# Eight experts' weights split into high and low halves: most low halves made by TensorE and ScalarE instead of VectorE

## The reference

```python
xf = x.reshape(-1, d)                            # 4096 tokens, d = 512
logits = jnp.dot(xf, w_gate)                     # E = 8 experts
top_logits, top_idx = jax.lax.top_k(logits, 2)
weights = jax.nn.softmax(top_logits, axis=-1)
sort_order = jnp.argsort(top_idx.reshape(-1))    # token copies grouped by expert
h0 = jax.lax.ragged_dot(sorted_x, wi_0, group_sizes)   # wi_0, wi_1: 8 x 512 x 256
h1 = jax.lax.ragged_dot(sorted_x, wi_1, group_sizes)
out_sorted = jax.lax.ragged_dot(silu(h0) * h1, wo, group_sizes)  # wo: 8 x 256 x 512
out = weighted sum of the two copies of each token
```

## Time and profile before

| | |
|---|---|
| time, median of 3 runs | 2045.12 us (2044.48 to 2049.25) |
| time of the profiled execution | 2043.97 us |
| its span in the profile | 2042.3 us |
| PE busy | 1773.9 us, 87% |
| DVE busy | 1737.6 us, 85% |
| ACT busy | 1341.5 us, 66% |
| POOL busy | 856.5 us, 42% |
| `route`, first instruction to last | 1606.8 to 1689.7 us of the span |
| `run_experts` | 1691.2 us to the end |

### The profile page before, as it was taken

How to read it: one execution, slowest core, us unless ns; L and a number is a source line. 1 busy time by engine, 2 the same in 40 slices (tenths; PEclk the granted TensorE clock), 3 DMA queues, 4 the chain that set the end, 5 groups by cost and what they waited for, 6 DMA issues and landing times. The chain is left out here.

```text
span 2042.3 us, 59210 instructions
## 1 busy us (share of the span) xinstructions
PE 1773.9 (87%) x24267; PEld 1226.2 (60%) x24326; DVE 1737.6 (85%) x2331; ACT 1341.5 (66%) x1933; POOL 856.5 (42%) x842
## 2 busy tenths in 40 slices
PE   3799999998999998999989999999984137999996
PEld 2567667666766676666667666767762013555553
DVE  6699999999999999999998999999994595666665
ACT  5478778877877787788768777868774332322322
POOL 5033422743282246227432822451234003766776
PEclk9899999999999999999999999999996568999998
DMA  6313424551554354445524553533332354566775
GB/s 190 112 39 83 113 67 83 127 138 45 113 128 117 68 124 127 99 83 120 143 47 102 128 126 71 124 102 82 73 67 83 105 156 140 184 203 216 247 260 190
DMA packets 205999, 246.30 MB, mean 121 GB/s; under 512 B 93668, under 2 KB 134628, under 8 KB 205728
## 3 DMA queue, kind: packets, MB, share of 16 engines
q1 hardware_dynamic: 165904, 146.43, 26.6%
q0 software_dynamic: 37952, 95.47, 18.2%
q10 hardware_dynamic: 1872, 0.55, 0.1%
HBM read 137.66 MB, written 70.79 MB: 102 GB/s over the span
## 5 line engine op out<-in xcount | busy, mean ns | idle before, releaser
L877 DVE TENSOR_TENSOR a_p_low<-a_p 128x1024 f16<-128x1024 f32 (+1 forms) x896 | 1095.6, 1248 | 91.7 <-ACT a_p L707 80.1
L707 ACT ACTIVATE a_p<-ps_s 128x1024 f32<-128x1024 f32 (+1 forms) x896 | 860.1, 965 | 284.1 <-PE ps_s L504 278.5
L504 PE MATMUL ps_s<-a_q_stack,a_k_stack 96*128 96x512 f16 (+1 forms) x1664 | 513.5, 383 | 13.7 <-ACT a_p L707 12.7
L630 PE MATMUL ps_o<-a_v,a_p 128*128 128x65 f16 (+1 forms) x6656 | 448.0, 195 | 44.2 <-ACT a_o_sums L735 21.4
L630 PE MATMUL ps_o<-a_v,a_p_low 128*128 128x65 f16 (+1 forms) x6656 | 447.2, 194 | 0.0
L630 PEld LDWEIGHTS ps_o<-a_v,a_p 128*128 128x128 bf16 (+1 forms) x6656 | 352.2, 98 | 143.5 <-DVE a_p_low L877 53.1
L541 PEld LDWEIGHTS ps_p<-wkv,a_ctx 128*128 128x128 f16 x4992 | 321.5, 98 | 143.5 <-DVE a_v L892 38.1
L541 PE MATMUL ps_p<-wkv,a_ctx 128*128 128x128 f16 x4992 | 365.7, 221 | 28.0 <-DVE a_v L892 26.7
L523 PE MATMUL ps_p<-a_ctx,wkv 128*128 128x384 f16 (+2 forms) x1536 | 349.9, 334 | 0.0
L630 PEld LDWEIGHTS ps_o<-a_v,a_p_low 128*128 128x128 f16 (+1 forms) x6656 | 317.7, 98 | 0.0
L523 PEld LDWEIGHTS ps_p<-a_ctx,wkv 128*128 128x128 f16 x1536 | 148.4, 98 | 140.4 <-issue 4.1
(11 more groups left out here) (242 smaller groups left out, 1996.4 us busy)
## 6 DMA issues: line engine op xcount, KB each, us to landing
a_k_stack<-a_k_parts SPq DMA_DIRECT2D x378, 80.0 KB, 2.2
d_ys<-f_y SPq DMA_DIRECT2D x71, 256.0 KB
a_ctx_raw<-in_ctx_dram POOLq DMA_DIRECT2D x64, 192.0 KB, 3.4
a_q_stack<-d_q_t SPq DMA_DIRECT2D x96, 128.0 KB, 4.1
a_xm<-in_x_dram SPq DMA_DIRECT2D x8, 1024.0 KB, 5.9
a_ctx_raw<-in_ctx_dram POOLq DMA_DIRECT2D x32, 256.0 KB, 4.2
d_q_t<-a_q_parts SPq DMA_DIRECT2D x32, 256.0 KB, 2.9
d_q_full<-a_xm SPq DMA_DIRECT2D x32, 256.0 KB, 2.8
```

What stands on the lines that cost most here:

```text
L504: mm = pe.matmul(t["ps_s"][s % 2][0:r, n * N:(n + 1) * N], t["k_stack"][v % 2][0:TERMS * DH, j, kt * P:kt * P + r], t["q_stack"][v % 2][0: ...
L630: mm = pe.matmul(t["ps_o"][:, q * VC:(q + 1) * VC], part[0:r, n * N + q * P:n * N + (q + 1) * P], val, start=(g == 0 and n == 0 and low == ...
L707: act.activation(t["p"][s % NP][0:r, 0:len(tiles) * N], t["ps_s"][s % 2][0:r, 0:len(tiles) * N], ACT.Exp, scale=float(DH) ** -0.5 / WSCALE ...
L877: dve.tensor_tensor(t["p_low"][s % NP][0:r, 0:n], full, high, ALU.subtract).then_inc(lows, 1)
```

## The change

The number of raw buffers goes from 3 to 4. Of the 24 low parts, VectorE keeps 8: pieces 3 and 17 to 23. The 16 others (0, 1, 2 and 4 to 16) are made in PSUM: for each half of a piece, TensorE multiplies the raw float32 half by a diagonal matrix of 64 in float32 and adds the high part times minus the identity in float16 (`subtract`), and ScalarE copies the result from PSUM to the low part as float16 (`low_piece`). Two PSUM tiles take turns, each two banks wide. GpSimd makes the two diagonal matrices at the stage's start. All engines' orders are written anew, and the stage has four semaphores more (20, were 16). Cut to its core:

```diff
-        raw = [sbuf(nc, held, f"e_raw{n}", [P, 2, 2 * FF], F32) for n in range(PIECES)]
+        raw = [sbuf(nc, held, f"e_raw{n}", [P, 2, 2 * FF], F32) for n in range(NW)]      # NW = 4
+ON_VECTOR = (3,) + tuple(range(17, PIECES * E))
+ON_TENSOR = [i for i in range(PIECES * E) if i not in ON_VECTOR]
...
+        def wait_read(eng, i):
+            if i in ON_VECTOR:
+                eng.wait_ge(split_vector, ON_VECTOR.index(i) + 1)
+            else:
+                eng.wait_ge(subtracted, ON_TENSOR.index(i) + 1)
...
+            pool.tensor_scalar(spread_32[:, :], k["id32"][:, :], WSCALE, None, ALU.mult).then_inc(diagonal, 1)
+            pool.tensor_scalar(minus_16[:, :], k["id32"][:, :], -1.0, None, ALU.mult).then_inc(diagonal, 1)
...
+            for i in range(PIECES * E):          # SyncE
+                if i >= NW:
+                    wait_read(sp, i - NW)
...
+            def high_piece(i):                   # ScalarE
+                act.wait_ge(loaded[i % NW], 32 * (i // NW + 1))
+                act.mul(weight_piece(i, 0), raw[i % NW][:, :, :], WSCALE).then_inc(high, 1)
+            def low_piece(j):
+                act.wait_ge(subtracted, j + 1)
+                act.copy(weight_piece(ON_TENSOR[j], 1), ps_low[j % 2][:, :, :]).then_inc(split_tensor, 1)
+            ready = iter(range(len(ON_TENSOR)))
+            def pieces(first, last):
+                for i in range(first, last):
+                    high_piece(i)
+                    if i in ON_TENSOR and ON_TENSOR.index(i) >= 1:
+                        low_piece(next(ready))
...
+            pieces(0, 3)
             act.wait_ge(gap_ready, 1)
             act.activation(ratio[:, :], gap[:, :], ACT.Exp, scale=1.0 / WSCALE).then_inc(ratio_ready, 1)
-            high_pieces(range(0, 4))
+            pieces(3, 13)
             for c in range(TOPK):
                 act.wait_ge(tile_ready, TOPK)
                 act.activation(mark(c, 0), tile_hot[c], ACT.Identity,
                                scale=row_1[:, 0:1]).then_inc(marked[c], 1)
-                high_pieces(range(4 + 2 * c, 6 + 2 * c))
+            pieces(13, PIECES * E)
+            for j in ready:
+                low_piece(j)
...
+            def subtract(j):                     # TensorE
+                i = ON_TENSOR[j]
+                pe.wait_ge(high, i + 1)
+                if j >= 2:
+                    pe.wait_ge(split_tensor, j - 1)
+                for h in range(2):
+                    pe.matmul(ps_low[j % 2][:, h, :], spread_32[:, :], raw[i % NW][:, h, :], start=True, stop=False)
+                    last = pe.matmul(ps_low[j % 2][:, h, :], minus_16[:, :], weight_piece(i, 0)[:, h, :], start=False, stop=True)
+                last.then_inc(subtracted, 1)
+            pe.wait_ge(diagonal, 2)
+            for j in range(3):
+                subtract(j)
             pe.wait_ge(hot_ready, 1)
...
+            for j in range(3, 12):
+                subtract(j)
             for c in range(TOPK):
                 pe.wait_ge(marked[c], 2)
...
+                for j in (range(12, 14) if c == 0 else range(14, len(ON_TENSOR))):
+                    subtract(j)
```

More of the change, by code:

```diff
@@ L1589 @@
 PIECES = 3
+NW = 4
+ON_VECTOR = (3,) + tuple(range(17, PIECES * E))
+ON_TENSOR = [i for i in range(PIECES * E) if i not in ON_VECTOR]
 VALUES = 6
@@ L1597, in route, with weight_piece @@
     with ExitStack() as held, phase(nc) as (block, sem):
-        raw = [sbuf(nc, held, f"e_raw{n}", [P, 2, 2 * FF], F32) for n in range(PIECES)]
-        loaded = [sem(f"e_loaded{n}") for n in range(PIECES)]
-        high, split = sem("e_high"), sem("e_split")
-        def weight_piece(e, n, part):
-            return t["wi"][:, e, part, 2 * n:2 * n + 2, :] if n < 2 else t["wo"][:, e, part, :, :]
+        raw = [sbuf(nc, held, f"e_raw{n}", [P, 2, 2 * FF], F32) for n in range(NW)]
+        loaded = [sem(f"e_loaded{n}") for n in range(NW)]
+        high, subtracted, split_tensor, split_vector, diagonal = (
+            sem("e_" + n) for n in ("high", "subtracted", "split_tensor", "split_vector", "diagonal"))
+        spread_32, minus_16 = sbuf(nc, held, "e_spread", [P, P], F32), sbuf(nc, held, "e_minus", [P, P], F16)
+        def weight_piece(i, part):
+            e, n = i // PIECES, i % PIECES
+            return t["wi"][:, e, part, 2 * n:2 * n + 2, :] if n < 2 else t["wo"][:, e, part, :, :]
+        def wait_read(eng, i):
[3 more added lines that the diff above has]
+                eng.wait_ge(subtracted, ON_TENSOR.index(i) + 1)
         sb = lambda name, shape, dt=F32: sbuf(nc, held, "r_" + name, shape, dt)
@@ L1645, in route @@
         ps_before, ps_total, ps_table = banks(nc, held, ["r_pb", "r_pt", "r_ps"])
+        ps_low = [held.enter_context(nc.psum_tensor(f"e_ps{n}", [P, 2, 2 * FF], F32)) for n in range(2)]
         made, spread, step, hot_ready, summed, gap_ready, ratio_ready, tile_ready, listed = (
@@ L1660, in _ @@
                                pattern=[[1, P]], channel_multiplier=-1).then_inc(made, 1)
+            pool.tensor_scalar(spread_32[:, :], k["id32"][:, :], WSCALE, None, ALU.mult).then_inc(diagonal, 1)
+            pool.tensor_scalar(minus_16[:, :], k["id32"][:, :], -1.0, None, ALU.mult).then_inc(diagonal, 1)
         @block.sync
         def _(sp):
[L1664 to L1674, removed]
+            for i in range(PIECES * E):
+                e, n = i // PIECES, i % PIECES
+                if i >= NW:
+                    wait_read(sp, i - NW)
+                for h in range(2):
+                    if n < 2:
+                        sp.dma_start(raw[i % NW][:, :, h * FF:(h + 1) * FF],
+                                     (t["wi_0"], t["wi_1"])[h][e, n * 2 * P:(n + 1) * 2 * P, :]
+                                     .rearrange("(c p) f -> p c f", p=P)).then_inc(loaded[i % NW], 16)
+                    else:
+                        sp.dma_start(raw[i % NW][:, h, :], t["w_out"][e, h * P:(h + 1) * P, :]).then_inc(loaded[i % NW], 16)
@@ L1676, in _ @@
         @block.scalar
         def _(act):
[L1678 to L1682, removed]
+            def high_piece(i):
+                act.wait_ge(loaded[i % NW], 32 * (i // NW + 1))
+                act.mul(weight_piece(i, 0), raw[i % NW][:, :, :], WSCALE).then_inc(high, 1)
@@ L1693, in _ @@
                                scale=row_1[:, 0:1]).then_inc(marked[c], 1)
-                high_pieces(range(4 + 2 * c, 6 + 2 * c))
+            pieces(13, PIECES * E)
+            for j in ready:
+                low_piece(j)
         @block.tensor
         def _(pe):
+            def subtract(j):
[3 more added lines that the diff above has]
+                    pe.wait_ge(split_tensor, j - 1)
+                for h in range(2):
+                    pe.matmul(ps_low[j % 2][:, h, :], spread_32[:, :], raw[i % NW][:, h, :], start=True, stop=False)
[4 more added lines that the diff above has]
+                subtract(j)
             pe.wait_ge(hot_ready, 1)
@@ L1707, in _ @@
                                      start=(c == 0 and n == 0), stop=(c == TOPK - 1 and n == TT - 1))
-            last.then_inc(listed, 1)
+                if c == TOPK - 1:
+                    last.then_inc(listed, 1)
+                for j in (range(12, 14) if c == 0 else range(14, len(ON_TENSOR))):
+                    subtract(j)
         @block.vector
@@ L1712, in _ @@
             done = Steps(dve, step)
-            pieces = iter([(e, n) for e in range(E) for n in range(PIECES)])
+            lows = iter(ON_VECTOR)
             def low_pieces(count):
                 flat = lambda a: a.rearrange("p a b -> p (a b)")
[L1717 to L1721, removed]
+                for i in itertools.islice(lows, count):
+                    dve.wait_ge(high, i + 1)
+                    dve.scalar_tensor_tensor(out=flat(weight_piece(i, 1)), in0=flat(raw[i % NW][:, :, :]),
+                                             scalar=WSCALE, in1=flat(weight_piece(i, 0)), op0=ALU.mult,
+                                             op1=ALU.subtract).then_inc(split_vector, 1)
             for n in range(TT):
@@ L1744, in _ @@
             dve.tensor_scalar(spare[:, :], row_1[:, :], float((TT - 1) * P), None, ALU.add)
-            low_pieces(3)
+            low_pieces(1)
             dve.wait_ge(summed, 1)
@@ L1754, in _ @@
                 src, dst = dst, src
-            low_pieces(2)
             done(dve.tensor_scalar(tiles[:, :], src[:, TT - 1, :], float(P - 1), 1.0 / P, ALU.add, ALU.mult))
@@ L1817, in _ @@
             dve.wait_ge(tile_ready, TOPK)
-            low_pieces(1)
             for c in range(TOPK):
@@ L1835, in _ @@
             dve.tensor_copy(t["expert_of"][:, :], of_tile[:, :])
-            low_pieces(3)
+            low_pieces(len(ON_VECTOR))
             dve.wait_ge(listed, 1)
@@ L1855, in _ @@
             done(dve.tensor_scalar(t["slot_weight"][:, :], t["slot_weight"][:, :], 1.0 / WSCALE, None, ALU.mult))
-            low_pieces(E * PIECES)
 NX = 6
```

## The result

The changed kernel took 2041.66 us (median of 20 runs, 2038.42 to 2048.46), the kernel before 2047.62 us in the same 20 rounds: ratio 0.9979, 95% interval 0.9971 to 0.9987, or 4.3 us less (2.7 to 5.9). The two medians by themselves lie 6.0 us apart, at the upper edge of that interval; I go by the ratio. The profiled execution took 2039.16 us with a span of 2037.4.

A forecast was written before the change was run, and what follows sets the result against it. The prediction took VectorE's list to bound `route`. Its schedule ended the stage 3.9 us earlier, plus 0.3 for semaphores: -3.6 us, from 2045.12 to 2041.5 us, range 2036.8 to 2049.5.

The forecast's parts named there:

- What bounds the stage before: `route`: bound by VectorE's list, idle gaps rare (0.77 and 0.55 us); 16 low parts taken away are 18.2 us of work.
- The subtraction: TensorE's price per piece, two float32 and float16 halves: 2.25 us at full clock, 4.1 us at clock 0.50.
- Weight loads exposed: Rival: weight loads on TensorE don't hide, a subtraction costs 3.2 us, end about 8 us later, 2049.5; chance 0.07.
- Head: Start of `route` up to L1748: routing gets there at 1623.2 instead of 1623.64, gaining 0.4 us; the rest becomes waits.
- Middle: From L1748 to the end of L1815: 18.9 us stay of 26.5; one-hot tiles ready 8.0 us earlier.
- Tail: Tables, last subtractions, loads and low parts, then the table's chain: ends at 1685.8 instead of 1689.68, 3.9 us earlier.
- loads bind: Rival: pieces 19 to 23 need 5.1 us to land at 2.1 spacing, end 2.7 us later, 2044.2; chance 0.12.
- the tail runs better: Rival: first table at full clock, subtractions 2.16 us, loads a microsecond sooner; end 3.6 us lower, 2037.9; chance 0.20.
- Semaphores: Stage's end: clearing four more semaphores costs at most 0.11 us each; 0.3 us taken for the four.
- The slow clock stays: Rival: waits keep TensorE at clock 0.50, each subtraction costs 4.1 us, total 2072.7 us; chance 0.06.

The follow-up runs named there:

- the second run: The changed kernel unaltered, run once more: stage 81.26 us (79.70 in its first run), ratio to the kernel before 0.9986 (0.9971 to 1.0002).
- the experiment: The kernel before with 16 semaphores added that nobody uses: stage 84.68 us against 84.5; VectorE's idle at the stage's end 2.78 us against 1.75.

## Why the prediction was right, point by point

The forecast was 2041.5 us, -3.6; the time was 2041.66, and the difference that was measured -4.3 (2.7 to 5.9 less). That the times agree within 0.2 us is luck: the forecast started from 2045.12, the median of three runs, and the kernel before had 2047.62 in twenty. What was right is the difference. Times below are from the stage's start, which the prediction had at 1606.76.

- **What bounds the stage before.** Half right. VectorE's list was the bound, but it wasn't as tight as I wrote. I named idle gaps of 0.77 and 0.55 us; the waits add up to 5.4. The largest, 2.8 for ScalarE's mark, isn't in the prediction at all, though one view of who waits for whom shows it.
- **The subtraction.** Right. 4.1 us at slow clock were forecast and the first took 3.95 to the start of the next (1612.15 to 1616.10): its first half 2.26, its second 1.69, as the clock rose within it. At full clock the starts of halves are 1.07 apart, so 2.15 a piece, and 2.24 with the short waits for ScalarE (subtractions 3 and 11 began at 1621.53 and 1639.43); I had 2.25 for the work alone.
- **Weight loads exposed.** Refuted. At full clock the float32 loads take 186 to 190 ns and the float16 ones 96 to 98. The Trainium skill, "TensorE: Matmul & The Clock Gate", section "Weight-path perf modes — Fast Weight Load (FWL) and DoubleRow", has the fast load off for float32; the trace agrees in direction. But the float32 matmul of a half takes 0.86 us, four times the 0.216 of a float16 one, so no load shows. (The rival's price for it, 8 us, was too high too: its own steps give about 7.)
- **Head.** L1748's place was forecast 16.4 us into the stage and came at 15.8, and in the second run at 16.8. In the kernel before it came at 16.9, so 1.1 us were gained (0.1 in the second run) where 0.4 were forecast. The start of low part 3 waited for ScalarE 1.21 us (2.24 in the second run), where the forecast's times give 1.8: half or more of the 2.3 us that were taken off there turned into that wait, as forecast.
- **Middle.** The 18.9 us hold (15.80 to 34.6). TensorE idled 5.15 us ahead of the first table (5.1 forecast).
- **Tail.** The chain of causes is the forecast's, link for link. The load of piece 19 went out behind subtraction 14, and the chain was the last work. The first table took 7.4 us to the next subtraction, not 8.3, since the clock rose sooner. VectorE waited 14.02 us (15). The load of piece 21 was mis-sized: it took 5.2 us from issue to ScalarE's start on it (1670.32 to 1675.52), where I allowed 4.2. It had been asked for 1.1 us behind piece 20 (1669.21); that this is the cause wasn't tested. Pieces 22 and 23 then came 1.5 and 1.3 us apart, where I had 1.7. So the rival *loads bind* had the time of piece 21 about right (5.1) and the spacing wrong. The stage's last work ended at 77.65 us, forecast 79.0, thus 5.3 us earlier than before, forecast 3.9: the earlier head, the table, subtractions of 2.15 us and the closer spacing of the last loads, part of the rival *the tail runs better*, outweighed piece 21.
- **Semaphores.** 0.3 forecast, 0.26 by the experiment; the gap at the end grew by 0.5 in the trace, of which 0.2 go with the chain as the last work.
- **The slow clock stays.** Refuted: the window from 1630 to 1640 has clock 1.00.
- **The cause of the gain.** Here the reasoning fell short while the number was right. I wrote that of 18.2 us taken off VectorE some 4 arrive, and of the fourth buffer only that "the four buffers hold": it had no term of its own. The buffer alone gives 4.3 and the moved low parts alone 0.4, both against a mark that may be nearly 1 us too high. I had never asked what the buffer does to the kernel before. The sum came out because it followed the new schedule as a whole, and a schedule's end doesn't say to which edit it is due. That part of the agreement isn't luck; the sentence on whose gain it is was wrong.

What stays open: why single executions of one kernel differ by 1.5 us in this stage. The parts that I could see are the landing of pieces 0 to 2, the point at which the clock rises (first table 7.5 to 8.0 us in the changed order), and the landing of the last loads.

## What to carry to other kernels

When a change has several parts, price each part alone against the kernel before, above all the small one that only seems to support the others; here one more buffer gave as much as the whole change. Add up all waits of the bounding engine before calling its list full, and look at what stands ahead of each step in the list of the engine that it waits for: a small step of the critical chain that is queued behind bulk work inherits the bulk's waits. When work is moved to another engine, its place in that engine's list decides what arrives: the same 16 subtractions gave 0.4 us or 11.9 us with three buffers, by the order of TensorE's and ScalarE's lists.

## What the runs showed of the hardware

- A float32 matmul of 512 columns with its float16 partner takes 1.07 us at full clock: 0.86 for the float32 one, as long as four float16 ones of 0.216; the slow float32 weight loads (0.19 us) are hidden under it.
- Filling 5 us of TensorE's idle with needless matmuls shortened the following set of 32 from 7.52 to 6.24 us, and an idle of only 2.33 us left it at 6.24.
- A load of 512 KB took 3.6 us from issue to ScalarE's start on it where nothing was under way (piece 3 of the kernel before), and 5.2 and 5.9 where it was issued 1.1 us behind another (piece 21 of the changed kernel and of the one with TensorE kept busy).
- Clearing a semaphore at a stage's end costs 0.064 us (16 more cost 1.03, one more 0.06).
